# Attention with a mixed feed-forward on one core: turned y stored once for batches 1 to 3, gate values and first weight mixes placed inside the gate stage

## The reference, cut to what matters

```python
# x: 4 batches of 2048 tokens, 512 features
x = x + layernorm(attention(layernorm(x)))             # windowed, 16 heads
# gate, one set of 8 values for each batch
y = layernorm(x)
h = relu(y @ gate_w1.T + gate_b1)
g = (h @ gate_w2.T + gate_b2).mean(over the batch's tokens)
mW1, mW2 = W1 + sum_e g[e] * TW1[e],  W2 + sum_e g[e] * TW2[e]
mb1, mb2 = b1 + g @ Tb1,  b2 + g @ Tb2
out = gelu(y @ mW1.T + mb1) @ mW2.T + mb2              # 2048 hidden features
x = x + layernorm(out)
```

## Time and profile before

| | us |
|---|---|
| median of 3 runs | 2894.65 (2893.51 to 2895.97) |
| profiled execution, device time | 2897.68 |
| its span in the trace | 2895.9 |
| PE busy | 2827.4 (98%) |
| DVE busy | 2061.3 (71%) |
| ACT busy | 1711.8 (59%) |
| POOL busy | 909.8 (31%) |
| PE busy in 1450 to 1500 us | 41.16 of 50 |

### The profile page before, as it was taken

One profiled execution on the slowest core, in us unless ns is written; L12 is line 12 of the kernel. 1 busy time (PEld: TensorE's weight loads), 2 busy tenths in 40 slices (PEclk: granted clock), 3 DMA queues, 4 the chain that ended last, 5 costly groups with the idle time before them and its releaser, 6 DMA issues.

```text
span 2895.9 us, 54593 instructions
## 1 busy us (share of the span) xinstructions
PE 2827.4 (98%) x19884; PEld 2361.3 (82%) x19884; DVE 2061.3 (71%) x3808; ACT 1711.8 (59%) x3325; POOL 909.8 (31%) x809
## 2 busy tenths in 40 slices
PE   7999999999999999989989999999999999999998
PEld 6888888888888888777768888788888888878886
DVE  5444444598998999888778666976678676796664
ACT  2222222377777776755546666766668666776666
POOL 2111111289888988954300000500005000130003
PEclk9999999999999999999999999999999999999999
DMA  6776777577877777679998667976579575895642
GB/s 240 239 242 233 240 249 261 189 212 220 231 211 206 205 209 216 192 274 402 394 397 315 228 225 248 365 284 201 200 283 401 204 252 201 299 361 204 217 139 88
DMA packets 340885, 722.30 MB, mean 249 GB/s; under 512 B 27536, under 2 KB 98320, under 8 KB 338720
## 3 DMA queue, kind: packets, MB, share of 16 engines
q1 hardware_dynamic: 304160, 629.40, 64.8%
q0 software_dynamic: 15024, 55.64, 5.5%
q10 hardware_dynamic: 21456, 34.05, 3.4%
HBM read 549.05 MB, written 167.84 MB: 248 GB/s over the span
## 4 chain that ended last, share of the span: by engine, by line
PE 83%; DVE 6%; DMA 4%; issue 3%; ACT 2%; POOL 2%; ACTq 0%; SPq 0%; DVEq 0%; POOLq 0%
PE a_acc L611 17%; PE e_acc L1427 7%; PE e_hid L1410 7%; PE e_acc L1428 7%; PE e_hid L1411 7%; PE e_acc L1429 7%; PE e_hid L1412 7%; PE a_ps_score L660 7%; PE a_ps_keys L677 6%; PE a_ps_out L698 5%; DMA a_gate_att<-o_scratch 2%; PE a_ps_out L706 2%; DVE e_part L1799 1%; PE a_ps_turn L716 1%; DVE a_gate_stats L1678 1%
## 5 line engine op out<-in xcount | busy, mean ns | idle before, releaser
L1799 DVE SCALAR_TENSOR_TENSOR e_part<-e_ring,e_g_cols,e_part 128x512 f32<-128x512 f32 x896 | 652.8, 783 | 4.9 <-DMA e_ring<-mix_rows 2.5
L529 DVE TENSOR_REDUCE a_neg_max<-a_ps_score 128x1 f32<-128x384 f32 (+1 forms) x1024 | 488.9, 529 | 86.2 <-PE a_ps_score L660 82.2
L1823 DVE TENSOR_TENSOR e_u_lo<-e_u,e_u_hi 128x512 fp32r<-128x512 f32 x256 | 179.2, 700 | 373.5 <-ACT e_u_hi L1558 373.4
L1554 ACT ACTIVATE e_u<-e_hid,e_mb 128x512 f32<-128x512 f32 x256 | 176.9, 691 | 431.2 <-PE e_hid L1412 419.6
L448 ACT ACTIVATE a_probs<-a_ps_keys 128x384 f32<-128x384 f32 (+1 forms) x1024 | 417.3, 480 | 20.4 <-PE a_ps_keys L677 9.4
L1283 POOL TENSOR_SCALAR e_var<-e_moments 128x4 f32<-128x4 f32 x15 | 6.8, 450 | 1283.2 <-DVE e_moments L1835 1282.7
L356 POOL TENSOR_TENSOR a_total<-a_probs 128x512 f32<-128x512 f32 x256 | 324.0, 1284 | 97.9 <-ACT a_probs L448 97.8
L660 PE MATMUL a_ps_score<-a_k_st,a_q_st 96*128 96x384 f32 (+1 forms) x1024 | 328.5, 361 | 4.6 <-DVE a_neg_max L529 3.8
L677 PE MATMUL a_ps_keys<-a_q_st,a_k_st 100*128 100x384 f32 (+1 forms) x1024 | 314.7, 350 | 2.7 <-ACT a_probs L448 1.7
L366 POOL TENSOR_TENSOR a_total<-a_total,a_probs 128x512 f32<-128x512 f32 x224 | 287.2, 1284 | 43.5 <-ACT a_probs L448 39.8
L1571 ACT ACTIVATE e_sums<-e_acc 128x512 f32<-128x512 f32 x508 | 289.4, 595 | 8.2 <-PE e_acc L1429 8.2
(11 more groups left out here) (163 smaller groups left out, 6454.2 us busy)
## 6 DMA issues: line engine op xcount, KB each, us to landing
e_ring<-mix_rows SPq DMA_DIRECT2D x558, 512.0 KB, 5.4
qk_scratch<-a_qk SPq DMA_DIRECT2D x128, 512.0 KB, 4.9
a_k_st<-qk_scratch SPq DMA_DIRECT2D x180, 256.0 KB, 4.1
a_q_st<-qk_scratch SPq DMA_DIRECT2D x180, 256.0 KB, 4.1
v_scratch<-a_v SPq DMA_DIRECT2D x64, 256.0 KB, 3.1
a_v_sb<-v_scratch SPq DMA_DIRECT2D x64, 256.0 KB, 4.2
o_scratch<-a_out SPq DMA_DIRECT2D x128, 128.0 KB
x_scratch<-a_gate_x POOLq DMA_DIRECT2D x16, 1024.0 KB, 9.9
```

The costliest lines, as they stand in the source:

```text
L529: dve.tensor_reduce(neg_max[:, g % 2, i, h:h + 1], ps_score[y % TRIO][:, 0:(hi - lo) * WIN], AX_X, ALU.max, negate=True).then_inc(reduced, 1)
L1799: dve.scalar_tensor_tensor(out=part[:, n % 2, half, :], in0=ring[:, slot, :], scalar=g_cols[:, b, e:e + 1], in1=so_far, op0=ALU.mult, op1= ...
```

## The change

1. For chunks 4 to 15 the turned y is no longer stored as two parts. ACT copies it a second time from the turn banks into a new tile `whole` (`stage`, four instructions a chunk, two slots), and SP stores that one tile (1 MB) to `yf_dram`. The copy stands on ACT between relu 1 and the second root. PE may turn the next chunk when it is done (semaphore `staged`). DVE's `low` and ACT's `high` of these chunks stay, since the gate uses them.
2. `SLOTS` goes from 3 to 2. Chunks 0 to 3 are stored as before, so for chunks 2 to 5 `high(c)` waits for the landing of the store of chunk c - 2. Chunks 6 and later don't wait there; `stage(c)` waits for the store of chunk c - 2 instead.
3. In the feed-forward, ACT loads one DMA into `y_lo` for a chunk of the next batch; one and two steps later in its loop it copies halves of it to `y_hi` (128x1024 each), and DVE subtracts `y_hi` from `y_lo` in place, in two halves. That is 24 instructions on each engine, 8 at each boundary.
4. The small loads and the 18 first ring loads are issued by SP in iteration 8 rather than 10, ahead of the loads of chunks 14 and 15. The gate values of batch 0 are formed behind the products of chunk 10, the columns behind those of chunk 11; DVE mixes the first halves of blocks 0 and 1 in iterations 13 and 14.
5. The tiles of the first half blocks (`wa_hi`, `wa_lo`) lie where the two slots of `whole` lie: ACT's first `high_half` waits for the store of chunk 14, DVE's first `low_half` for that of chunk 15. DVE's order behind the gate is new, and PE runs `hidden(1)` ahead of `gate_values(1)`.

```diff
+        def stage(act, c):
+            if c >= PER + SLOTS:
+                await_yt(act, c - SLOTS)
+            for k in range(KD):
+                act.wait_ge(lo_done, KD * c + k + 1)
+                act.activation(whole[:, c % SLOTS, k, :], turn[k][:, :], ACT.Copy).then_inc(staged, 1)
...
                 if there(k):
                     relu(k, 1)
+                if there(k + 1) and k + 1 >= PER:
+                    stage(act, k + 1)
                 if there(k + 2):
                     take_sqrt(act, k + 2, 1)
...
+            def split_y(s):
+                for b, q, h in halves_due(s):
+                    if h == 0:
+                        act.wait_ge(y_loaded[q], 16 * (b + 2))
+                    at = slice(2 * h, 2 * h + 2)
+                    act.activation(y_hi[:, y_slot(q), at, :], y_lo[:, y_slot(q), at, :].bitcast(F32), ACT.Copy).then_inc(hi_done, 1)
...
                 if 2 <= s and s + AHEAD < STEPS:
                     low_hidden(s + AHEAD)
+                for b, q, h in halves_due(s + AHEAD):
+                    dve.wait_ge(hi_done, half_split(b, q, h))
+                    rows = y_lo[:, y_slot(q), 2 * h:2 * h + 2, :]
+                    dve.tensor_tensor(rows, rows.bitcast(F32), y_hi[:, y_slot(q), 2 * h:2 * h + 2, :], ALU.subtract).then_inc(lo_done, 1)
...
         def high(act, c, k):
-            if k == 0 and c >= SLOTS:
+            if k == 0 and SLOTS <= c < PER + SLOTS:
                 await_yt(act, c - SLOTS)
...
             def low_half(n, half):
+                if n == half == 0:
+                    await_yt(dve, CHUNKS - 1)
```

116 lines of the change are left out of this document (73 added, 43 removed).

## The result

The changed kernel takes **2928.9 us** (median of four runs, 2927.95 to 2932.99) against 2895.31 us for the kernel before on the same chip (2893.51 to 2897.99): a ratio of 1.0118, 95% interval 1.01 to 1.0135. That is 33.6 us slower, where 18.9 were forecast. The profiled execution has a span of 2926.2 us, 30.3 more than the one of before; what follows accounts for these 30.3.

The account below looks back on a forecast made before the run. A chain through DVE paces the gate stage, DMA second; the change acts only through PE's idle time and slow matmuls. 10.9 - 9.9 + 17.9 = +18.9 us on the 2894.65 median gives 2913 us, range 2893 to 2930.

Parts of the forecast that it names:

- my likeliest case: Whole kernel: the forecast of 2913 us itself, with 2903 to 2925 as its own range; chance 0.55.
- no relief: Gate stage or boundaries: `make_y` stays 3.09 us or subtractions wait for POOL; 2921 to 2931 us, chance 0.16.
- the relief: Gate stage: `make_y`, started later, meets only the end of POOL's adds and takes 1.92 us in place of 3.09.
- part 4: Batch boundaries: DVE's subtractions and ACT's copies make PE wait for `e_u_lo`, +8.3, +3.7 and +5.9, sum +17.9 us.
- Part 1: Gate stage: staging copies delay ACT's root 1.65 us, `make_y` ends 0.6 us later; a chunk takes 13.7 us.
- Part 2: Gate stage: `high(3)` waits for the store of chunk 1, 19.5 us in landing; DVE's next iteration starts 5.7 us later.
- I take no wait from it: Gate stage: SP's loads of chunks 14 and 15, behind 24 more DMAs, cost no wait, as bandwidth leaves room.
- Part 3: Way into the feed-forward: waits for gate values and batch sums go, `project(1)` starts 9.0 us earlier; together -9.9 us.
- just covered: Way into the feed-forward: chunk 15's store lands near 1457.5, before `hidden(0)` starts at 1459.6, so `low_half(0, 0)` costs nothing.
- this rival: Way into the feed-forward: chunk 15's store holds DVE, each microsecond past 1459 costs PE one; +5, 2918 us, chance 0.04.
- waits for `e_u_lo` near 24 us: Boundaries: PE's waits for `e_u_lo` total near 24 us in place of 6.2; under 12 us the forecast falls.
- absorbed: Boundaries: subtractions shift DVE to a time without POOL's adds; part 4 is +4, time 2900 us, chance 0.13.

Follow-up runs that it names:

- stage_behind_root: Changed kernel with the four staging copies of a chunk put behind ACT's second root instead of ahead of it; ratio 1.0115 to the kernel before.
- ring_late: Changed kernel with its 18 ring loads put back behind the loads of chunk 15, small loads still early; ratio 1.0093 to the kernel before.
- once_best: Changed kernel with ring loads late, staging copies behind the root, planner told of the halves, eight DVE mixes ahead of `low_half(0, 0)`; 2888.03 us, ratio 0.9979.
- planned: Changed kernel with the mix planner told of 1.25 us more DVE time in each of two steps per boundary; ratio 1.0024 to the kernel before.
- before_planned: Kernel before with only the planner's 1.25 us in two steps of each boundary added, as a control; ratio 0.9983 to the kernel before.
- no_subtract: Changed kernel without DVE's 24 subtractions, so with another output; ACT's copies and all waits stay; ratio 1.0002 to the kernel before.
- halves_early: Changed kernel with each half of y split one loop step earlier on ACT and DVE; ratio 1.0092 to the kernel before.
- store_first: Changed kernel with SP's ring refill and loads of y for chunks 0 and 1 put behind the store of chunk 15; ratio 1.0144 to the kernel before.

## Why the prediction was right in sign and too small

The kernel is slower, as forecast, and 2928.9 lies inside the range of 2893 to 2930, by 1.1 us, and above the 2903 to 2925 of my likeliest case. It lies where I had put the rival "no relief" (2921 to 2931), which is not what happened: the relief came. The sum was 18.9 us and the trace has 30.3, by parts: the gate stage +12.3 (forecast 10.9), the way into the feed-forward -9.4 (-9.9), the boundaries +27.4 (+17.9). Nearly all that is missing is in part 4, and the step that failed there is the price of the slow clock behind the new waits, which I had left out.

**Part 1, the staging copy: right, a little large.** The root came 1.56 us late (1.65 forecast), `make_y` lost its 1.10 us of company with POOL's adds, and the net was 0.46 us a chunk against the same kernel without the delay, 0.25 against the 13.19 of before; forecast 0.5. The relief came in full, as `stage_behind_root` shows by taking it away. The Trainium skill (SBUF — State Buffer, Who interferes with whom) has it that DVE and GpSimd lock each other out of the port pair they share; 1.98 against 3.08 us agrees.

**Part 2, two slots: right in kind, too large.** I took the landing of chunk 1's store at 19.5 us from the trace of before. In the kernel after it landed in 15.1 us: issued at 1269.61, it released `high(3)` at 1284.76. The wait of `high(3)` was 1.01 us and not 6, with 2.88 and 0.78 us at its neighbours, of which I had counted none. DVE's iteration at 1306.43 of before came at 1308.45, 2.0 us late where my sum had 6.3; 1.5 of that difference are the earlier start of this trace's gate stage.

**"I take no wait from it": wrong, 7.33 us.** This is the failed step of the gate stage. I held the bytes of the ring loads against the room left over three chunks, and they fit. But SP issues in order and 18 issues took 11.43 us, so the load of chunk 14 went out at 1394.97, 7.8 us late, and with the ring's bytes ahead of it landed in 15.0 us, not 6.3. `ring_late` takes both away. That the gate stage's 12.3 us came out near my 10.9 is luck, errors against each other: 4.3 us too much for the slots, 1.7 too much for the copies, 7.3 too little here.

**Part 3: right in sum, less so in its steps.** From `make_y` of chunk 14 to `project(1)` it is 59.1 us in place of 67.7, a gain of 8.6 where I had 9.0. The batch sums' wait went, the wait for the last mixes was 4.15 us (4 forecast), the one for the columns 0.64 (3 forecast). `project(1)` came 3.6 us later in the span than before, where I had said about 2; 1.4 of that are the gate stage. The store of chunk 15 was not "just covered": issued at 1459.21, since SP sat in the refill that waits for DVE's mixes, it held DVE for 9.44 us. PE felt 1.41 of them. I gave this rival 0.04; its mechanism came and its price did not: with DVE's wait for the store down to 2.63 us, `once_best` has the same 4.15 us ahead of `project(1)`.

**Part 4: the wrong instruction, the right idle time, and a price left out.** PE's idle time at the boundaries rose from 6.2 to 24.1 us, by 17.9, which is the forecast to the tenth. That is partly luck. It was to be waited for at `e_u_lo`; PE waits for the halves, which stand behind that `e_u_lo` on DVE and which `hidden` needs before `project` needs `e_u_lo`. By boundaries it was 8.4, 7.2 and 2.2 where I had 8.3, 3.7 and 5.9: at the second PE waits 3.50 and 3.71 us for halves, about twice my term, and why the cover that I had counted there was missing wasn't tested; at the third 6.0 us of new waits are only 2.2 more, as a stall of before, 3.79 us, was gone. The falsifier "waits for `e_u_lo` near 24 us" has to be read as failed, for it was 0: by my own test ("under 12 us") the forecast of part 4 falls, though the idle time is right.

The term that was mis-sized is the clock. The boundaries cost 27.4 us and not 17.9. In the windows above the granted clock is 0.94, 0.95 and 0.93 over 90, 70 and 70 us, 13.8 us of full clock lost; before it was 0.98, 1.00 and 0.97 over 81, 60 and 65 us, 3.6 lost. The difference of 10.2 is the missing 9.5, within rounding. The matmuls say the same without the rounded clock. At full clock one takes 0.226 us (200 us for 884, window of before below); the 869 of the three windows of before took 3.2 us more than that, the 854 of after 12.6 more. In part 3 I had counted 1.2 us for slow matmuls behind the new waits; in part 4, with seven waits of 1.2 to 6.4 us, nothing. Each microsecond of waiting cost about half a microsecond more, and the trace of before had this price ready: 6.2 us of waiting, 3.2 of slow matmuls.

**What the profile of before did not tell me.** I treated the halves as instructions added to a full list. `planned` shows that the list was not full, only in the wrong order: DVE is busy for 68% of the time between the boundaries (third number of the window of before below), the planner spreads the mixes by a budget of DVE's time, and this budget was not told of 1.25 us in two steps. With it, the halves cost 7.3 us (`planned` against `before_planned`); without it the subtractions alone cost 32.7 (no_subtract's -5.3 against +27.4). My rival "absorbed", with no change in the time, came only in `planned`, and mostly by the order of the mixes; a part by POOL's adds, as I had argued it, isn't excluded at the first boundary.

```profile
1600.00:1800.00 200.00, 200.00 (x884) 165.62 (x883) 136.19 (x198) 128.70 (x227) 0.00 (x0) 1.00 0.67 222
```

## What to carry to other kernels

When work is added to an engine whose order a planner's budget sets, look whether the budget counts it; if not, price the change twice, as it is and with the budget put right. Price a new wait of PE by its idle time and by the slow matmuls behind it, read from a window over a like wait. A load moved ahead in a queue is paid by what then stands behind it: for the next load that is wanted, add its later issue and its longer landing, and hold the sum against the time by which it used to be early. Whether the bytes fit over some chunks doesn't answer that.

## What the hardware did that I had not expected

POOL's four adds at the end of a batch come in two kinds, and DVE pays for one of them. In the kernel after, first boundary, POOL and then DVE:

```profile
1862.88 5.01 POOL L1318 TENSOR_TENSOR e_sums<-e_sums,e_x 128x512 f32<-128x512 f32 x4
```

```profile
1860.49 10.61 DVE L1849 SCALAR_TENSOR_TENSOR e_part<-e_ring,e_g_cols,e_part 128x512 f32<-128x512 f32 x6
```

and in `planned`:

```profile
1863.64 6.66 POOL L1319 TENSOR_TENSOR e_sums<-e_sums,e_x 128x512 f32<-128x512 f32 x4 [0.17 <-ACT e_sums L1637]
```

```profile
1863.95 3.50 DVE L1850 SCALAR_TENSOR_TENSOR e_part<-e_ring,e_g_cols 128x512 f32<-128x512 f32 x2
1867.37 4.81 DVE L1850 SCALAR_TENSOR_TENSOR e_part<-e_ring,e_g_cols,e_part 128x512 f32<-128x512 f32 x4
```

Where the adds run through in 5.0 us, 1.25 each, one mix of DVE takes up to 6.26 us where it else takes 0.74: it is held for all four. Where they take 6.4 to 7.6 us, no mix is held that long, and in `planned` none takes over 1.79. The first kind is there at the first and third boundary of the kernel before (adds of 5.02 and 4.99 us), and those are the two at which PE waits 2.44 and 3.79 us; at one boundary of the kernel after, at none of `planned` and `no_subtract`, at all three of `halves_early`. In the slower kind each series in these traces but the one at 2224.52 of the kernel after has a wait of POOL ahead of its first add. No series of the first kind has such a wait. What decides the kind was not tested by itself. It moves with edits made elsewhere: the third boundary of `ring_late` and the second of `store_first` and of `stage_behind_root` are of the first kind where the kernel after has the second, and they cost 1.9 to 2.0 us more in the table. And none of the fifteen boundaries of the five kernels with the planner's line is of the first kind, so that some of what the line brought may have come this way.
